# Attention inside a fused block on Trainium2: value tiles in runs of three instead of two

## The reference

```python
s = jnp.einsum('bthd,bshd->bhts', q, k) * scale
logits = DEG * jnp.log(jnp.abs(s) + 1e-30) + log_G[:, :, :, None] - log_G[:, :, None, :]   # DEG = 2, causal mask
a = jnp.where(mask, jnp.exp(logits - m), 0.0)
num = jnp.einsum('bhts,bshd->bthd', a, v)
den = jnp.sum(a, axis=-1)
y = num / (den[..., None] + 1e-06)
```

## Time and profile before

| | us |
|---|---|
| median of 3 executions | 2264.68 |
| lowest and highest | 2263.64, 2266.38 |
| the profiled execution | 2261.05 |
| its span | 2259.3 |
| TensorE busy in the span | 2019.7 |
| VectorE busy | 1788.5 |
| ScalarE busy | 1297.6 |
| GpSimd busy | 797.1 |

### The profile page before, as it was taken

One profiled execution on the slowest core, in us unless ns is written; L12 is line 12 of the kernel. 1 busy time (PEld: TensorE's weight loads), 2 busy tenths in 40 slices (PEclk: granted clock), 3 DMA queues, 4 the chain that ended last, 5 costly groups with the idle time before them and its releaser, 6 DMA issues. The chain is left out here.

```text
span 2259.3 us, 37985 instructions
## 1 busy us (share of the span) xinstructions
PE 2019.7 (89%) x13205; PEld 1383.3 (61%) x13205; DVE 1788.5 (79%) x2635; ACT 1297.6 (57%) x2169; POOL 797.1 (35%) x745
## 2 busy tenths in 40 slices
PE   7787856999999999999999999599934999999994
PEld 6565632444444444444444444499823999999994
DVE  5666644999999999999999999677759777777773
ACT  4333325777777777777777776244410666656661
POOL 4666640111111111111111111166616566666663
PEclk9888877999999999999999999699965999999997
DMA  5988887134444333444433340344431344444344
GB/s 175 236 209 219 201 211 166 46 91 122 117 117 121 76 88 91 122 117 117 122 77 87 90 122 15 91 129 130 129 128 46 81 87 86 85 86 87 82 85 106
DMA packets 173240, 259.39 MB, mean 115 GB/s; under 512 B 45576, under 2 KB 121040, under 8 KB 163152
## 3 DMA queue, kind: packets, MB, share of 16 engines
q1 hardware_dynamic: 145072, 213.94, 37.0%
q0 software_dynamic: 15840, 22.29, 6.2%
q10 hardware_dynamic: 12160, 20.97, 2.8%
HBM read 161.22 MB, written 100.14 MB: 116 GB/s over the span
## 5 line engine op out<-in xcount | busy, mean ns | idle before, releaser
L945 ACT ACTIVATE att_sb_a<-att_ps_s,att_sb_fg,att_sb_f 128x1024 f32<-128x1024 f32 x384 | 458.8, 1203 | 272.8 <-PE att_ps_s L1070 267.0
L981 DVE TENSOR_TENSOR keep_sb_store<-keep_sb_store,att_sb_a 128x1024 f32<-128x1024 f32 (+1 forms) x528 | 533.1, 1036 | 34.2 <-ACT att_sb_a L945 32.2
L904 POOL TENSOR_SCALAR_AFFINE_SELECT att_sb_dec<-att_sb_dec 128x128 f32<-128x128 f32 x256 | 129.4, 505 | 971.5 <-ACT att_sb_dec L935 971.5
L1070 PEld LDWEIGHTS att_ps_s<-first_sb_q,first_sb_k 64*128 64x128 f32 x1920 | 159.8, 186 | 172.1 <-issue 100.6
L1070 PE MATMUL att_ps_s<-first_sb_q,first_sb_k 64*128 64x512 f32 (+3 forms) x1920 | 248.3, 382 | 11.8 <-PEq L618 11.8
L1070 PEld LDWEIGHTS att_ps_s<-att_sb_q,att_sb_k 64*128 64x128 f32 x1920 | 158.9, 185 | 158.8 <-issue 86.5
L1718 ACT ACTIVATE ffn_sb_h<-ffn_ps_p,ffn_sb_b_cols 128x256 f32<-128x256 f32 x320 | 152.0, 477 | 168.9 <-PE ffn_ps_p L1909 168.9
L1070 PE MATMUL att_ps_s<-att_sb_q,att_sb_k 64*128 64x512 f32 (+3 forms) x1920 | 247.4, 381 | 0.0
L997 DVE SCALAR_TENSOR_TENSOR att_sb_a<-att_ps_s,att_sb_dec 128x1024 f32<-128x1024 f32 (+3 forms) x256 | 209.7, 819 | 39.5 <-PE att_ps_s L1070 35.3
L1823 DVE TENSOR_TENSOR ffn_sb_h_lo<-ffn_sb_h,ffn_sb_h_hi 128x256 fp32r<-128x256 f32 x320 | 212.8, 707 | 27.8 <-ACT ffn_sb_h_hi L1711 26.0
L1085 PE MATMUL att_ps_off<-att_sb_a,first_sb_v 128*64 128x512 f32 x768 | 198.3, 605 | 8.1 <-ACT att_sb_a L945 8.1
(11 more groups left out here) (255 smaller groups left out, 3846.0 us busy)
## 6 DMA issues: line engine op xcount, KB each, us to landing
q_rows<-early_sb_halves SPq DMA_DIRECT2D x128, 256.0 KB, 4.4
ffn_sb_raw<-L_ffn_W ACTq DMA_DIRECT2D x36, 512.0 KB, 4.1
close_sb_nT<-num_rows SPq DMA_DIRECT2D x34, 512.0 KB, 4.0
k_rows<-early_sb_halves SPq DMA_DIRECT2D x64, 256.0 KB, 4.2
att_sb_hb<-half_log SPq DMA_DIRECT2D x16, 1024.0 KB, 24.4
att_sb_q<-q_rows SPq DMA_DIRECT2D x16, 1024.0 KB, 14.3
att_sb_k<-k_rows SPq DMA_DIRECT2D x16, 1024.0 KB, 18.3
num_rows<-att_sb_num SPq DMA_DIRECT2D x64, 256.0 KB, 2.2
```

Of the source, the lines that this page charges most:

```text
L904: nc.gpsimd.affine_select(out=tile, in_=tile, compare_op=ALU.is_ge, fill=0.0, base=0, pattern=[[1, P]], channel_multiplier=-1).then_inc(de ...
L945: nc.scalar.activation(x, s_ps[slot(op)][:, :, :], ACT.Square, scale=f[:, p, i - 1, s:s + 1], bias=fg[:, p, i - 1, s:s + 1]).then_inc(sq_d ...
L981: nc.vector.tensor_tensor(x[:, :, c:TB], x[:, :, c:TB], y[:, :, c:TB], ALU.max).then_inc(max_done, 1)
L1070: last = nc.tensor.matmul(s_ps[slot(op)][:, h, c:TB], k_sb[p][at_h, a_k, key * P:(key + 1) * P], q_sb[p][at_h, a_q, i * TB + c:(i + 1) * T ...
```

## The change

Value tiles are numbered so that they fall behind every third place, whatever it is: `d + (2 - d) % 3 + 0.5` with d a whole number is half a place behind the next place that is 2 modulo 3. A value tile comes 2.5, 3.5 or 4.5 places behind its scores (5.5, 6.5 or 7.5 for own tiles), where it was 2.5 or 3.5 (5.5 or 6.5). Sums and totals are numbered 0.25 behind their last values and not 1.2.

```diff
     def values_at(op):
-        d = place[op] + (2.5 if op[1] == "off" else 5.5)
-        return d if int(d) % 2 else d + 1
+        d = place[op] + (2 if op[1] == "off" else 5)
+        return d + (2 - d) % 3 + 0.5
...
-    part_order = Order({(q, i): values_at(last_off(q, i)) + 1.2 for q, i in blocks})
-    total_order = Order({(q, i): values_at(last_own(q, i)) + 1.2 for q, i in owns})
+    part_order = Order({(q, i): values_at(last_off(q, i)) + 0.25 for q, i in blocks})
+    total_order = Order({(q, i): values_at(last_own(q, i)) + 0.25 for q, i in owns})
...
-    dve_todo += [(values_at(last_off(q, i)) + 1.2, "part", (q, i)) for q, i in blocks]
-    dve_todo += [(values_at(last_own(q, i)) + 1.2, "total", (q, i)) for q, i in owns]
+    dve_todo += [(values_at(last_off(q, i)) + 0.25, "part", (q, i)) for q, i in blocks]
+    dve_todo += [(values_at(last_own(q, i)) + 0.25, "total", (q, i)) for q, i in owns]
```

## The result

The changed kernel took 2268.97 us (median of 16 executions, 2266.28 to 2271.89) against 2264.53 for the kernel before (16 executions): ratio 1.0019, 95% interval 1.0012 to 1.0026. That is 4.4 us slower. The forecast was 1.1 us faster, which is "no change": the time lies in the stated range, but the kernel became slower, by a small amount that is clear of the scatter of the executions.

A forecast was written before the change was run, and what follows sets the result against it. TensorE was taken to bound the attention stage, with VectorE 92% busy. Terms -35.8 + 35.7 + 1.3 - 5.1 - 3.0 + 3.8 + 2 = -1.1 us gave 2263.6 us against 2264.68, range 2252 to 2278.

The forecast's parts named there:

- block 2 to block 3: Ten places where these blocks' `off` values meet in one run: TensorE waits 1.04 us each for sums, together 10.4.
- term 2: At 26 of 47 block borders, last and next first `off` values share a run; TensorE waits for sums: +35.7 us.
- term 3: Other attention-stage waits: totals -5.1, value tiles before new blocks -3.0, block 0 transposes awaiting maxima +3.8, score buffers +2 us.
- Term 1: Attention stage on TensorE: fewer turns between scores and values, 116 rounds less, partly offset by transpose borders: -35.8 us.
- the turns are not saved: Rival: each score tile pays its own turn, so the saving shrinks from 39.4 to 17; 2285 us, chance 0.03.
- Block 3 to block 1: Ten meetings of block 3 with the next pair's block 1: five wait 0.95 us, five 1.7; together 4.8 plus 8.5.
- Block 1 to block 2: Six meetings of these blocks: sums stand behind a maximum and an own-scores product; wait 2.0 us each, together 12.0.
- The restart: A value tile that has waited at a meeting begins like the first of a run: 26 x 0.05 = +1.3 us.
- the rival of a full 0.34: A run that has stood restarts like a full turn, 8.8 us in place of 1.3; 2271 us, chance 0.07.
- VectorE is ready: Rival: VectorE is at its post at every meeting, so their waits total 24.7; 2252.6 us, chance 0.27.
- VectorE becomes the queue: Rival: all meetings cost 2.0 us, 52 in total; decided from a mean wait of 1.6; 2280 us, chance 0.20.
- The signs: Traces would show turnless runs of three, some 26 sums waits of 1 to 2 us, and no L1016 wait.

The follow-up runs named there:

- e5: Kernel before the change, with values behind every place instead of every second; 2331.09 us, ratio 1.0295 to the kernel before.
- e6: Changed kernel with sums and totals numbered 0.21 ahead of their last values instead of 0.25 behind; 2260.2 us, ratio 0.9980 to the kernel before.
- e3: Changed kernel, a block's first `off` value tile moved one run later where it would join the previous block's last; 2227.13 us, ratio 0.9844 to before.
- e7: e3 with an empty 45th place per body, another phase of runs, and block 2's transposes two places later; 2216.81 us, ratio 0.9783 to before.

## Why the prediction was wrong

The mechanism was right: turns saved, and given back where two blocks meet. Two sizes failed, both in the same direction: the meetings, 2.9 us too low, 2.4 of them at block 2 to block 3 (term 2: 10.4 forecast, 12.8 measured), and the transposes, 2.8 too low (term 3: 3.8 forecast, 6.6 measured). Together that is 5.7 us, and the stage missed its forecast by 5.2. In both, TensorE was taken to arrive later than it did.

- **Term 1, turns, held.** -35.8 against -35.4, and the third score tile costs 0.68 where 0.70 was forecast. The rival "the turns are not saved" is refuted, by e5 from the other side too.
- **Term 2, meetings, held in kind and fell short in size**: +35.7 against +38.6. Block 3 to block 1 came out place by place, five at 0.96 and five at 1.71 (0.95 and 1.7 forecast). Block 1 to block 2 came out at 12.4 for 12.0 partly by luck: five places cost 2.19 and not 2.0, and the first, in pair 0, only 1.44. The step that failed is the one for block 2 to block 3, 12.8 against 10.4: five places cost 1.17 and five 1.40, where about 1.07 and 1.04 were read. The five at 1.40 are those with one more product ahead of the sums. One of them in the changed kernel, on TensorE:

```profile
919.89 0.44 PE L1085 MATMUL att_ps_own<-att_sb_a,first_sb_v 128*64 128x128 f32 x4
920.16 1.03 PE L1085 MATMUL att_ps_off<-att_sb_a,first_sb_v 128*64 128x512 f32 x4
922.42 1.08 PE L1085 MATMUL att_ps_off<-att_sb_a,first_sb_v 128*64 128x512 f32 x4 [1.24 <-DVE att_sb_part L1006]
923.43 0.50 PE L1070 MATMUL att_ps_s<-first_sb_q,first_sb_k 64*128 64x512 f32 x2
```

  and on VectorE:

```profile
919.36 1.22 DVE L997 SCALAR_TENSOR_TENSOR att_sb_a<-att_ps_s,att_sb_dec 128x1024 f32<-128x1024 f32 x1
920.49 0.41 DVE L981 TENSOR_TENSOR keep_sb_store<-keep_sb_store,att_sb_a 128x256 f32<-128x256 f32 x1
920.82 0.95 DVE L997 SCALAR_TENSOR_TENSOR att_sb_a<-att_ps_s,att_sb_dec 128x768 f32<-128x768 f32 x1
921.69 0.68 DVE L1006 TENSOR_TENSOR att_sb_part<-att_ps_off,att_sb_et 128x512 f32<-128x512 f32 x1
```

  The wait is 922.42 - 920.16 - 0.86 = 1.40, not 1.04. The same product before:

```profile
785.76 1.22 DVE L997 SCALAR_TENSOR_TENSOR att_sb_a<-att_ps_s,att_sb_dec 128x1024 f32<-128x1024 f32 x1
```

  VectorE's side was forecast rightly: the sums were forecast 2.34 behind it at 788.1, and they started 2.33 behind the product (921.69 - 919.36). TensorE's side was not: it could have gone on at 921.02 (920.16 + 0.86), 1.66 behind the same product, where 787.8 is 2.04 behind. So it arrives 0.38 earlier against VectorE than I had it. That is near the 0.34 of a saved round, which I had counted for block 3 and for the other five places here (the 786.9) and left out of the 787.8. That the saved round is the cause is my reading of the sizes; no run tests it alone.
- **The restart** was priced rightly at an ordinary turn: the tile that had waited took 1.01 until 923.43, as the lone one of the earlier trace rows, and so did the other 25. The rule of the Trainium skill that was weighed there ("TensorE: Matmul & The Clock Gate", Single matmul latency), by which 0.166 us would be paid anew, does not show at these places, and neither does the rival of a full 0.34.
- **Term 3, the transposes, missed most for its size**: +3.8 against +6.6. The place in block 0:

```profile
887.71 0.70 PE L1070 MATMUL att_ps_s<-att_sb_q,att_sb_k 64*128 64x384 f32 x6
889.35 1.06 PE L1058 MATMUL att_ps_s<-keep_sb_ident,keep_sb_store 128*128 128x128 f32 x8 [0.94 <-DVE keep_sb_store L981]
```

```profile
888.78 0.41 DVE L981 TENSOR_TENSOR keep_sb_store<-keep_sb_store,att_sb_a 128x256 f32<-128x256 f32 x1
```

  The maximum ends at 889.19 and the transposes start 0.16 later, where I had taken the 0.06 of the earlier trace rows. That makes 0.1 of the difference; the wait is 1.0 and not 0.75, and the rest fits a saved turn on the way (0.17). Besides, the transposes of block 2, which I had not looked at, wait 0.3 in one body of three, 1.5 us in all, and the last transposes of the stage wait 1.2 once.
- **What went** (-9.5 against -8.1) and the **score buffers and the rest** (+2.5 against +2, inside 0 to 5) are near.
- **The rivals.** "VectorE is ready" did not come about: the meetings cost 38.6 and not the floor of 24.7, for the reason that e6 shows, the instructions ahead of the sums. "VectorE becomes the queue" did not come about either: the mean wait at the 26 places is 1.5 us, under the 1.6 from which it was to decide, VectorE was 91% busy in the three bodies and not 95%, and e3 and e7 run faster yet with VectorE at 93 and 94%.
- **The signs.** What was to show the forecast right came, all of it: 26 waits of 0.96 to 2.2 us, their sum between 25 and 50, TensorE's busy time 2.1 us lower per body and its idle time 2.3 higher, no wait for L1016. They tell the mechanism from its rivals, but not a gain of 1 us from a loss of 4. The terms missed by up to 3 us each in a sum made of 36 less 36, and that was enough for the wrong sign.

## What to carry to other kernels

When two kinds of work alternate on the bounding engine, longer runs save a fixed price per turn, but a run that holds both the last use and the next first use of one buffer makes this engine wait for the whole round trip to its reader; look for such meetings in the order before running, since moving one tile by one run at each of them turned a loss of 4 us into a gain of 34. And if a change is a large gain less a large loss, forecast the difference only with the clock moved on all engines, for each turn saved can bring the bounding engine to a hand-off earlier than its partner.

## What the runs showed that was not expected

- Transposes that wait for VectorE start 0.15 us after the end of the instruction that releases them, in every such wait of the changed kernel (12) and of e3 (22), while value tiles that wait for the sums follow VectorE by 0.055 us. Both are TensorE waiting for VectorE; what makes the difference was not tried.
- The stages behind the attention, where all these kernels are alike, took 834.2 to 841.2 us in the profiled executions (834.5 before, 838.0 and 840.2 in two executions of the changed kernel). A single pair of profiles can therefore not carry a statement about 4 us of the whole; the stage's own length came out 4.1 and 3.6 us over before in the two.
